# Attention of 8 sequences as one pipeline of 16 steps per sequence, with the softmax sums inverted from PSUM

## What is computed

```python
q = (hidden_states @ q_w.T + q_b).reshape(b, s, H, HEAD_DIM)     # H = 16, HEAD_DIM = 32
k = hidden_states @ k_w.T + k_b
v = hidden_states @ v_w.T + v_b
scores = jnp.einsum('bqhd,bkd->bhqk', q, k) / HEAD_DIM ** 0.5
scores = jnp.where(causal[None, None], -jnp.inf, scores)
attn = jax.nn.softmax(scores.astype(jnp.float32), axis=-1)
out = jnp.einsum('bhqk,bkd->bqhd', attn, v).reshape(b, s, H * HEAD_DIM)
return out @ o_w.T + o_b
...
x = x + _layernorm(_L0_attn_ref(_layernorm(x)))
x = x + _layernorm(_L0_ffn_ref(_layernorm(x)))
```

## Time and profile before

| | us |
|---|---|
| median of 3 runs | 2210.64 |
| lowest and highest | 2209.67, 2216.05 |
| the profiled execution | 2211.64 |
| its span, first to last instruction | 2209.9 |
| attention stage in it | 0 to 829 |
| routing | 829 to about 897 |
| experts | about 897 to 1446 |
| shared stage | 1446 to 2210 |

### The profile page before, as it was taken

How to read it: one execution, slowest core, us unless ns; L and a number is a source line. 1 busy time by engine, 2 the same in 40 slices (tenths; PEclk the granted TensorE clock), 3 DMA queues, 4 the chain that set the end, 5 groups by cost and what they waited for, 6 DMA issues and landing times. The chain is left out here.

```text
span 2209.9 us, 32623 instructions
## 1 busy us (share of the span) xinstructions
PE 2059.7 (93%) x11754; PEld 1604.8 (73%) x11754; DVE 1141.1 (52%) x2253; ACT 704.0 (32%) x1254; POOL 465.8 (21%) x885
## 2 busy tenths in 40 slices
PE   5999999999999953799999999989999999999995
PEld 4666676766667633677788788878888888888884
DVE  4766758577675738444445555444433424334243
ACT  3425345353543420344444444332111111111111
POOL 1323414142341420211101111001012021120212
PEclk9999999999999975899999999999999999999998
DMA  5043261414415112444434545333022020220202
GB/s 172 31 119 114 62 174 38 136 54 120 128 48 153 39 57 79 172 156 154 154 141 180 211 143 195 109 105 100 19 76 95 19 76 19 76 95 19 76 20 95
DMA packets 104418, 222.76 MB, mean 101 GB/s; under 512 B 9472, under 2 KB 23552, under 8 KB 101152
## 3 DMA queue, kind: packets, MB, share of 16 engines
q1 hardware_dynamic: 92832, 184.14, 25.4%
q0 software_dynamic: 11520, 37.76, 5.4%
HBM read 157.37 MB, written 62.91 MB: 100 GB/s over the span
## 5 line engine op out<-in xcount | busy, mean ns | idle before, releaser
L1121 PE MATMUL ex_bank<-ex_xT,ex_gu 128*128 128x512 f32 (+14 forms) x1656 | 345.1, 367 | 5.4 <-DVE ex_xT L1155 5.4
L1121 PEld LDWEIGHTS ex_bank<-ex_xT,ex_gu 128*128 128x128 f32 (+1 forms) x1656 | 276.8, 182 | 69.9 <-DVE ex_xT L1155 5.9
L1171 DVE TENSOR_TENSOR sh_silu<-sh_silu,sh_bank 128x512 f32<-128x512 f32 x88 | 60.5, 688 | 444.6 <-ACT sh_silu L1164 444.6
L627 DVE TENSOR_REDUCE at_nmax<-at_bank 128x1 f32<-128x384 f32 (+3 forms) x512 | 216.5, 472 | 108.3 <-PE at_bank L431 108.2
L777 ACT ACTIVATE at_PT<-at_bank 128x512 f32<-128x512 f32 (+1 forms) x384 | 187.5, 526 | 265.0 <-PE at_bank L483 258.6
L1121 PE MATMUL sh_bank<-sh_xT,sh_gate 128*128 128x512 f32 x1056 | 256.3, 392 | 4.1 <-DVE sh_xT L1155 4.1
L1133 PE MATMUL sh_bank<-sh_dn,sh_act 128*128 128x512 f32 x1056 | 255.1, 390 | 0.0
L1121 PE MATMUL sh_bank<-sh_xT,sh_up 128*128 128x512 f32 x1056 | 253.9, 389 | 0.0
L837 POOL TENSOR_TENSOR at_minus_max<-idf,at_nmax 128x512 fp32r<-128x512 f32 x128 | 134.1, 1048 | 503.2 <-DVE at_nmax L627 484.9
L1164 ACT ACTIVATE sh_silu<-sh_bank 128x512 f32<-128x512 f32 x88 | 52.6, 598 | 586.4 <-PE sh_bank L1121 586.4
L1121 PEld LDWEIGHTS sh_bank<-sh_xT,sh_gate 128*128 128x128 f32 x1056 | 199.8, 189 | 45.9 <-DVE sh_xT L1155 4.3
(11 more groups left out here) (229 smaller groups left out, 2818.7 us busy)
## 6 DMA issues: line engine op xcount, KB each, us to landing
ex_gu_in<-gu_in SPq DMA_DIRECT2D x23, 1408.0 KB, 9.3
at_Qs<-q_dram SPq DMA_DIRECT2D x96, 256.0 KB, 5.7
ys<-sh_yk SPq DMA_DIRECT2D x17, 1024.0 KB, 5.7
q_dram<-at_q_h SPq DMA_DIRECT2D x64, 256.0 KB, 4.1
ex_dn_in<-dn_in SPq DMA_DIRECT2D x23, 512.0 KB, 9.9
at_x_in<-x_in SPq DMA_DIRECT2D x8, 1024.0 KB, 9.6
at_x_res<-x_in SPq DMA_DIRECT2D x8, 1024.0 KB, 6.6
x<-at_y SPq DMA_DIRECT2D x8, 1024.0 KB, 8.4
```

The lines of the kernel that those rows point to most:

```text
L627: last = nc.vector.tensor_reduce(nmax[:, s % 3, i:i + 1], S_ps[u][:, col:col + (i + 1) * P], AX_X, ALU.max, negate=True)
L1121: last = self.nc.tensor.matmul(self.gate_up_ps[c % 2][which][0:m, 0:w], cols(i, k), self.xT[j][:, k, 0:w], start=(step == 0), stop=(step = ...
L1171: nc.vector.tensor_tensor(silu[c % 2][0:m, 0:w], silu[c % 2][0:m, 0:w], gate_up_ps[c % 2][1][0:m, 0:w], ALU.mult).then_inc(s["product"], 1)
```

## The change

The attention loop is rewritten as a pipeline of 16 steps per turn, 10 turns in all (8 sequences and two to drain). In step s of turn b PE does: a transpose of the maxima of head s-1 (L389), the query scores of head s (L402), a first filler, the first part of a group's sums or values, a second filler, the rest of that group, and the key scores of head s-2 (L419). ACT exponentiates head s-3.

- The maximum enters the key scores as a 97th row of `Qs` against a row of ones in `KsT`: the four maxima columns are transposed by PE to a 4x128 tile in bank 3, copied by ACT (`take_row`), and moved into `Qs` by a DMA that ACT issues (`move_row`). POOL's diagonal matrix and the L483 matmuls are gone, and so are the mask matmuls of the key scores; POOL zeroes the masked part of `PT` afterwards in two `affine_select`s per head (`mask_later_keys`).
- The end of the turn is gone. Its parts are fillers, all in bank 7: q projections in steps 12, 13, 15 and 0; second norm's transposes in 1 and 2; router product in 3; logits and V transposes in 4; output projection in 5 to 8; transposes of x in 9 and 10; the v and k projection in 11.
- Sums are made in steps 1, 3, 9 and 13, values in steps 2, 4, 10 and 14, both in bank 3. The transpose of the maxima of the next step, in the same bank, waits for `sums_taken` or `mixed_taken`.
- DVE inverts the sums in four `RECIPROCAL`s in a row (`take_sums`). The low half of the mixed values goes from DVE to POOL. Keys are kept twice (`KsS`, `KsT`); ACT issues their six moves.
- The attention stage also stores both halves of the transposed second norm (`xnT`, 2 MB a sequence). The shared stage loads these halves, two sequences ahead at the start, and neither transposes nor splits.

```diff
+        SUM_STEP = {9: 0, 13: 1, 1: 2, 3: 3}
+        MIX_STEP = {10: 0, 14: 1, 2: 2, 4: 3}
+        Q_STEP = {12: 0, 13: 1, 15: 2, 0: 3}
...
+            def transpose_maxima(n, h):
+                pe.wait_ge(max_ready, 3 * (H * n + h) + 3)
+                nc.tensor.transpose(AV_ps[0:QT, 0:P], nmax[:, h % 2, :], idf[:]).then_inc(rows_ps, 1)
...
+            def key_scores(n, h, before):
+                if h == 0:
+                    pe.wait_ge(kT_moved, 48 * n + 48)
+                pe.wait_ge(row_moved[h % 2], 8 * H * n + 16 * (h // 2) + 16)
+                for tb, tiles in enumerate(T_UNITS):
+                    if has(before[0]):
+                        pe.wait_ge(pt_ready, 3 * (H * before[0] + before[1]) + tb + 1)
...
+            def turn(b):
+                for s in range(H):
+                    n, h = head(b, s, 1)
+                    if has(n):
+                        m, g = group(b, s - 1, SUM_STEP)
+                        k, f = group(b, s - 1, MIX_STEP)
+                        if g is not None:
+                            pe.wait_ge(sums_taken, C * m + g + 1)
+                        elif f is not None:
+                            pe.wait_ge(mixed_taken, C * k + f + 1)
+                        elif has(head(b, s, 2)[0]):
+                            pe.wait_ge(row_taken, H * head(b, s, 2)[0] + head(b, s, 2)[1] + 1)
+                        transpose_maxima(n, h)
+                    if has(b):
                         query_scores(b, s)
...
+                    first_filler(b, s)
+                    begin_values(b, s)
+                    second_filler(b, s)
+                    end_values(b, s)
+                    transpose_v(b, s)
+                    n, h = head(b, s, 2)
+                    if has(n):
+                        key_scores(n, h, head(b, s, 3))
...
+            def take_sums(b, s):
+                n, g = group(b, s, SUM_STEP)
+                if g is not None:
+                    dve.wait_ge(summed, C * n + g + 1)
+                    for i in range(QT):
+                        last = nc.vector.reciprocal(over_sum[:, i * P:(i + 1) * P], AV_ps[:, i * P:(i + 1) * P])
+                    last.then_inc(sums_taken, 1)
...
+                    maximum(b, s, 0)
+                    norm_steps(b, s, 0)
+                    maximum(b, s, 1)
+                    norm_steps(b, s, 1)
+                    first_low(b, s)
+                    maximum(b, s, 2)
+                    norm_steps(b, s, 2)
+                    second_low(b, s)
+                    take_sums(b, s)
+                    scale_mixed(b, s)
+                    take_v(b, s)
+                    norm_steps(b, s, 3)
...
+                    exponentials(b, s, 0)
+                    if s == 2 and has(b) and has(b - 1):
+                        act.wait_ge(shifted, 3 * H * b)
+                        move_k(b, KsT, kT_moved)
+                    take_row(b, s)
+                    high_mixed(b, s)
+                    exponentials(b, s, 1)
+                    move_row(b, s)
+                    first_high(b, s)
+                    exponentials(b, s, 2)
+                    second_high(b, s)
+                    if s == H - 1 and has(b + 1):
+                        act.wait_ge(scores, 3 * H * (b + 1))
+                        move_k(b + 1, KsS, kS_moved)
```

More of the change, by code:

```diff
@@ new lines, in second_filler, with transpose_v @@
+            def second_filler(b, s):
+                if s in (1, 2) and has(b - 2):
+                    normed_to_columns(b - 2, b, 2 * s - 1)
+                if s in (9, 10) and has(b + 1):
+                    x_to_columns(b + 1, 2 * s - 17)
+            def transpose_v(b, s):
+                if s == 4 and has(b):
+                    if has(b - 2):
+                        pe.wait_ge(lg_ready, b - 1)
+                    pe.wait_ge(qkv_lo, 5 * b + 5)
+                    for j in range(QT):
+                        last = nc.tensor.matmul(F_ps[:, j * HD:(j + 1) * HD], vk[0:HD, j * P:(j + 1) * P],
+                                                idf[0:HD, 0:HD], start=True, stop=True)
+                    last.then_inc(v_ps, 1)
@@ L626, in maxima, with maximum @@
+            for c in range(C - 1):
+                low_q(0, c, bank[1 + c])
+            def maximum(b, s, u):
+                if not has(b):
+                    return
+                dve.wait_ge(scores, 3 * (H * b + s) + u + 1)
                 for i, col in S_UNITS[u]:
-                    last = nc.vector.tensor_reduce(nmax[:, s % 3, i:i + 1], S_ps[u][:, col:col + (i + 1) * P],
+                    last = nc.vector.tensor_reduce(nmax[:, s % 2, i:i + 1], S_ps[u][:, col:col + (i + 1) * P],
@@ new lines, in turn @@
+            def turn(b):
+                for s in range(H):
+                    if s == 6 and has(b + 1):
+                        norm[0].refine(b + 1)
+                    if s == 10 and has(b - 1):
+                        norm[1].refine(b - 1)
+                    if s == 12 and has(b - 1):
+                        add_residual(b - 1, 2)
+                        add_residual(b - 1, 3)
+                    low_mixed(b, s)
+                    mask_later_keys(b, s)
+                    if s == 11 and has(b - 1):
+                        add_residual(b - 1, 0)
+                        add_residual(b - 1, 1)
+                    if s == 14 and has(b - 1):
+                        norm[2].refine(b - 1)
@@ L1493, in turn @@
                 sp.dma_start(seq(out, b), f[:]).then_inc(stored, 16)
[L1495 removed]
+            pairs(sp, turn)
             sp.wait_ge(stored, 16 * NB)
@@ L1559, in turn @@
                         normalize(b - 1)
-                if not last:
-                    for c in range(C):
-                        high_x(nc, b + 1, c, xT, gate_up_ps, s)
                 act.wait_ge(scales_ready, b + 1)
```

937 lines of the change are left out of this document (462 added, 475 removed).

## The result

The changed kernel takes 2404.09 us (median, 2400.37 to 2405.60), the kernel before 2211.55 in the same comparison: a ratio of 1.086 (95% interval 1.085 to 1.088). The change makes the layer 193 us slower. The forecast was 2360, range 2265 to 2430.

What follows compares the result with a forecast made beforehand. The prediction took PE's own work to bound the kernel before. On the profiled 2211.6 us it put +97 for the attention's new chain, +64 for clock falls and -11 for the shared stage: 2361, taken as 2360, range 2265 to 2430.

Steps and rivals of the forecast that it cites:

- the signs I gave: Trace signs of being right: turns 107 to 118 us, PE 75 to 85% busy, 3 us idle behind reciprocals, clock 0.8 to 0.95.
- The bound and the new chain: Attention turn: PE bound before; afterwards steps wait on PE, ACT and DVE hand-overs, 102.8 us a turn, 107 with ACT's issues.
- The clock: Attention turns: PE's waits lower the granted clock, seven falls a turn at 1.2 us, 53 falls in all, +64 us.
- PE's own work: Attention turn: PE's work falls by 14.2 to about 76.5 us, with a head taking 1.6 instead of 2.49.
- ACT's issues: DMAs issued by ACT in the attention: 0.6 us each, together 4.2 a turn, including 1.6 in step 2 and 1.3 at step 0.
- ACT as the engine that PE waits for: Attention: PE waiting for ACT's list was named as a sign that the forecast is wrong; no size given.
- The row's DMA: Move of the maxima's row: about 7 us available against 2.0 to land, so hidden; PE's key scores waiting for it meant wrong.
- Shared stage: Stage after attention: loses its transposes, 1.6 us a turn in seven turns on PE's path, 11 us less.
- Start and drain: Ends of the attention stage: turn 0 takes 75 us, turn 1 97, draining 85 against 58 before.
- Without the clock: Rival for the whole kernel: the chain's waits but no clock falls, 2297 us, or 2268 with free issues; chance 0.20.
- Slower still: Rival for the whole kernel: nine or more falls at 1.7 us, or clock staying low, 2404 up to 2480; chance 0.11.
- PE stays the bound: Rival: hand-overs under 0.7 us, only sum steps wait, 88.5 us a turn, about 2175 to 2190 in all; chance 0.09.

Runs made afterwards that it cites:

- run 2: Changed kernel with eight matmuls that nothing reads added on PE in each of the four sum steps, inside the wait for the inversions: 2336.36 us, ratio 1.056.
- Run 6: Changed kernel with ACT issuing the query-score keys' three copies right behind step 15's row, ahead of that step's high half and third exponential: 2359.41 us, ratio 1.065.
- Run 10: Changed kernel with sums copied out and inverted between maxima, third maximum ahead of the low half, and keys moved earlier: 2224.16 us, ratio 1.005.
- run 1: Changed kernel with three of the four inversions of each group left out, so the output is not the layer's: 2262.18 us, ratio 1.023.
- run 8: Four-edit version with step 2's row taken before the key moves, two normalizations moved to step 0, and inversions placed later, against that version: 2261.78 us, ratio 1.022.
- the query bank: Changed kernel with the maxima transposed into the third query-score bank instead of the bank of the sums: 2345.11 us alone, ratio 1.059.
- runs 7: Changed kernel with four edits: sums copied out, third maximum first, maxima transposed into the third query-score bank, keys moved earlier: 2256.96 us, ratio 1.019.

## Why the prediction was right, and where it was short

The time lies in the range, the direction and the mechanism hold, and the 44 us that are missing are nearly all in one term, the clock's. Of the signs I gave, PE is busy 81% of a turn, waits about 3 us for DVE behind the reciprocals and in eight other steps of a turn for the reductions, at a granted clock of 0.87; the turns of 121 us are beyond the 118 I allowed.

- **The bound and the new chain: right.** PE's transpose of the maxima waits for DVE as the steps were worked out. The spacing of two starts of L389 gave, in the turn from 615.00, sum steps 3 and 13 of 9.9 each (9.5 forecast), sum steps 1 and 9 of 8.6 and 8.8 (8.9 with ACT's issues), output tiles of 5.0 to 5.1 (5.1), q and v/k steps 15, 12 and 11 of 6.1, 6.0 and 6.7 (5.9, 5.9 and 6.9). The turn without its low time is 106.8 us; the forecast of the chain with ACT's issues was 107. What is over it stands in five steps: the values, each behind a sum step or the next one, took 8.7 (step 2), 9.4 (4), 7.5 (10) and 6.0 (14) where I had 7.55, 6.05, 6.25 and 4.2, and step 0 took 11.6 for 7.2. That is 11.9 us in this turn; the other eleven steps together are 0.4 over the forecast. In the four value steps it is the clock: where run 2 leaves it up they take 5.9, 6.1, 5.9 and 4.4.
- **The clock: right cause, the term mis-sized.** I put seven falls a turn at 1.2 us each, 8.4. The four turns have fewer, 5.5 stretches each, but of 5.7 us on average; that is 31 us at half clock and 14.4 us lost, 2.6 for each. Over the stage the changed kernel has 280 us of low time and the kernel before 38: (280 - 38) x 0.46 = 111 us, where the forecast has 64. The difference, 47, is the miss of 44. What I had too short is the length of a stretch, 3.4 us from the earlier trace rows; the number of falls I had too high, which hid part of it. Of the 22 stretches nine last 3 to 3.5 us, twelve 6.5 or 7 and one 14, and it isn't a second wait that makes them long: in none of them does PE begin a new wait of over 0.1 us. In step 4 of the turn from 615.00 PE resumes at 642.24 after 2.76 us of idling, and is then busy at half clock throughout:

```profile
643.50:650.00 6.50, 6.50 (x43) 3.43 (x42) 1.59 (x6) 0.38 (x1) 0.77 (x2) 0.50 0.00 0
```

The kernel before had shown both lengths. I measured the stretch after the second wait of the earlier trace rows; after the first it is 7 us (with one wait of 0.46 in it):

```profile
44.50:51.50 7.00, 6.54 (x26) 4.75 (x26) 3.36 (x8) 1.58 (x3) 2.07 (x2) 0.51 1.07 270
```

Why one stretch lasts twice as long as another stays open: steps 4 and 14 both follow a wait of about 2.75 us, with 6.5 and 3.5 us at half clock.

- **PE's own work: too low, without effect.** 76.5 us a turn were forecast. In the version whose turns are nearly free of falls PE is busy 339.12 / 4 = 84.8. Each head takes 1.8 (transpose and query scores 1.0, key scores 0.75), not 1.6, and four transposes 0.6, not 0.43; that is 4.6 of the 8.3, and where the rest lies I did not look. In the changed kernel most steps are set by the chain, so the error hardly shows.
- **ACT's issues: right in size, wrong in place.** One issue takes 0.6 us, as taken. But step 0 took 11.6 us against 7.2: the keys' copies are issued behind the high half of step 15, PE has them 4.4 us after the first issue (721.18 to 725.55) and waits 2.40 for them, and the projection then runs at half clock. Run 6 priced it, 45 us for the kernel. I had charged the issues to ACT's list and forgotten that PE's first scores wait for their landing. For step 2, on the other hand, I charged 1.6 us for the three issues ahead of the row, and they cost nothing: ACT issues them from 620.59 on, while PE still waits for the inversions, and at full clock (run 2) the step takes 5.9, which is the forecast without the 1.6. The two errors cancel in the turn, so that 106.8 meets 107 so closely is partly luck.
- **ACT as the engine that PE waits for** was a sign of being wrong, and it is there, though small: 22.4 us for exponentials (L812 in the list of waits), which stand on ACT's list behind the filler's high half. In the four turns it is 2.4 us a turn, 0.6 in each of steps 11, 12, 15 and 0, and in each of these a wait for DVE follows, so the chain decides there all the same.
- **The row's DMA: hidden, right.** No wait for it is among those of PE's list shown above.
- **Shared stage: 11 forecast, 11.8 measured.**
- **Start and drain.** From the last normalization in the loop to the last logits I had 85 us; it is 1031.57 - 948.26 = 83.3. The first two turns took 202.5 us (42.1 to 244.65), where I had 172 and 17 for the clock. They hold 65.5 us of low time, 30 us by the rate, so their chain was right too and the 14 us more belong to the clock's 47.
- **The rivals.** Without the clock (2297) is refuted by run 2: matmuls that nothing reads took 68 us away. "Slower still" (2404 and more) had the clock stay low longer than I took, which it does, but because the next wait comes too soon, which it doesn't; its lower end is the time measured. "PE stays the bound" asked that the hand-overs take less than 0.7 us. They don't (output tiles take the 5.1 us of the chain). Run 10, with three edits, comes nearest to it, but at 95.4 us a turn where it had 88.5, and no faster than the kernel before.

The Trainium skill ("TensorE: Matmul & The Clock Gate", the section on psum-queue depth-cycling) tells of PE idling shortly between groups of matmuls that cycle through PSUM banks, and of throughput lost to the clock going down and up. The trace agrees: 22 stretches in four turns, and 68 us back when four waits a turn were filled. The estimate of 1.0 us for four inversions, worked out from the Trainium skill's table ("VectorE: DVE Perf Modes", TRN2 errata), is not borne out: the trace has 3.39. With three of the four inversions left out (run 1) the kernel is still 48 us slower than before, so by that figure too the change would have been a loss.

**What stays open.** Why the third query scores still wait 27 us for the row in run 8, and which part of the query bank's cost is the row and which the clock (13.4 against 2.6 us low a turn between runs 7 and 10), was not taken apart. And no version beats the kernel before: with turns of equal length, run 10 still reaches its last logits 21.6 us later (850.24 against 828.69), of which the shared stage gives 10.5 back. From the normalization at 686.42 to the last logits it takes 163.8 us against 136.4 before, the drain through the one filler bank; that was seen, not tested.

## What to carry to other kernels

When a pipeline is made to hand one bank from PE to a slow engine and back each step, cost every step as a chain through the engines and not by busy time, and let the slow engine first empty the bank by a copy and do its work between other steps; here that edit was worth 106 us. Waits on PE cost their length and then again by the clock: measure the stretch at the lower level behind every such wait of the trace at hand, not behind one, since here they lasted 3.5 or 7 us after waits of the same length. And price edits in the company in which they will stand: one that gained 59 us alone lost 33 in the version with the others.

## What I had not expected of the hardware

- Adding 256 matmuls of 512 columns whose result nothing reads made the kernel 68 us faster, since idling 0.84 to 1.25 us in place of 2.75 to 3.2 left the clock up in most sum steps (low time 35 instead of 125 us in four turns).
- A stretch of low clock lasted 6.5 to 7 us, without a further wait of PE, as often as 3 to 3.5 (12 and 9 of 22).
- A fill that stopped 7.55 us before the wait ended kept nothing: the transposes behind it ran at 1.11 us for four, the same as after 21 us of idling.
- Waits of 1.5 to 2.0 us three times a turn, in the three-edit version, brought only three stretches of low clock in four turns: behind waits of 1.84, 1.85 and 2.00, not behind another of 1.85. The waits of the earlier trace rows of 1.4 to 1.6 us were each followed by one. The length of a wait alone doesn't tell whether the clock falls.
